# A fused cross-attention and FFN kernel on one core: four reorderings around GEGLU, CROSS2 and FFN

## The reference

```python
# first block: 16 heads of 64
x = attn(LN(x), LN(x), Wq1, Wk1, Wv1, Wo1, bo1) + x          # SELF
x = attn(LN(x), context, Wq2, Wk2, Wv2, Wo2, bo2) + x        # CROSS
h = LN(x) @ Wp + bp;  a, gate = split(h, 2)
x = (a * gelu(gate)) @ Wf + bf + x                           # GEGLU
# second block: 16 heads of 8
out = attn8(x @ Wq + bq, context @ Wk + bk, context @ Wv + bv) @ Wo + bo    # CROSS2
out = out + gelu(LN(out) @ W1 + b1) @ W2 + b2                # FFN
return x + out
```

## Time and profile before

| | |
|---|---|
| median of 3 runs | 451.03 us (450.54 to 451.25) |
| the profiled execution's own time | 450.97 us |
| its span, first to last instruction | 449.3 us |
| TensorE matmuls (PE) | 434.4 us, 97% of the span |
| VectorE (DVE) | 352.9 us, 79% |
| ScalarE (ACT) | 318.8 us, 71% |
| GpSimd (POOL) | 201.8 us, 45% |
| granted TensorE clock | 1.00, the higher of its two levels (2.4 GHz) |

### The profile page before, as it was taken

One profiled execution on the slowest core, in us unless ns is written; L12 is line 12 of the kernel. 1 busy time (PEld: TensorE's weight loads), 2 busy tenths in 40 slices (PEclk: granted clock), 3 DMA queues, 4 the chain that ended last, 5 costly groups with the idle time before them and its releaser, 6 DMA issues.

```text
span 449.3 us, 17107 instructions
## 1 busy us (share of the span) xinstructions
PE 434.4 (97%) x7513; PEld 399.4 (89%) x7513; DVE 352.9 (79%) x649; ACT 318.8 (71%) x587; POOL 201.8 (45%) x226
## 2 busy tenths in 40 slices
PE   8999999999999999999999999999999999999897
PEld 7979999898999999989989899889999777778797
DVE  4888889688797887978978789896784788898471
ACT  5686676777778768787677776876546576777763
POOL 1883332555345634555352533523342232152782
PEclk9999999999999999999999999999999999999999
DMA  7202021110200000000000000000000000000011
GB/s 230 58 4 85 3 85 28 53 48 4 63 4 4 10 3 11 12 3 10 12 2 12 3 10 13 3 3 1 2 1 19 10 12 19 4 1 4 13 36 47
DMA packets 14623, 10.61 MB, mean 24 GB/s; under 512 B 5188, under 2 KB 13592, under 8 KB 14552
## 3 DMA queue, kind: packets, MB, share of 16 engines
q1 hardware_dynamic: 14120, 9.48, 7.3%
q10 hardware_dynamic: 432, 0.07, 0.1%
HBM read 8.50 MB, written 1.05 MB: 21 GB/s over the span
## 4 chain that ended last, share of the span: by engine, by line
PE 88%; DVE 6%; ACT 2%; issue 2%; POOL 1%; DMA 1%; POOLq 0%
PE stage L683 12%; PE stage L684 11%; PE stage L685 11%; PE scp L865 8%; PE scp L788 7%; PE scp L837 6%; PE scp L944 6%; PE out0p L885 4%; PE out0p L913 4%; PE out0p L887 3%; PE out0p L886 3%; PE stage L849 3%; PE scp L805 2%; DVE pr L1417 1%; PE stage L934 1%
## 5 line engine op out<-in xcount | busy, mean ns | idle before, releaser
L1734 POOL TENSOR_TENSOR pr<-pr,rc 128x1024 f32<-128x1024 f32 (+1 forms) x32 | 59.1, 1867 | 76.5 <-DVE rc L1447 76.4
L1165 ACT ACTIVATE pr<-pr 128x1024 f32<-128x1024 f32 x48 | 50.8, 1059 | 36.7 <-DVE pr L1417 30.1
L1672 POOL TENSOR_TENSOR rstd<-veps,neghalf 128x2 f32<-128x2 f32 x32 | 22.8, 714 | 70.8 <-DVE veps L1365 70.6
L1099 ACT ACTIVATE vt<-stage 64x512 f32<-64x512 f32 x83 | 49.2, 592 | 4.8 <-PE stage L685 1.2
L1461 DVE COPY vt<-stage 64x512 f32<-64x512 f32 x45 | 31.2, 694 | 21.8 <-PE stage L685 20.9
L1412 DVE TENSOR_REDUCE mx<-scp 128x16 f32<-128x1024 f32 x32 | 39.2, 1224 | 8.9 <-PE scp L788 8.5
L1099 ACT ACTIVATE ot_h<-scp 128x512 fp32r<-128x512 f32 x64 | 33.4, 600 | 13.3 <-PE scp L865 13.3
L1467 DVE TENSOR_TENSOR ot_r<-scp,ot_h 128x512 fp32r<-128x512 f32 x64 | 40.0, 683 | 2.3 <-ACT ot_h L1099 1.0
L1099 ACT ACTIVATE k_of_heads<-stage 128x512 f32<-128x512 f32 x62 | 36.9, 598 | 5.4
L1417 DVE TENSOR_TENSOR pr<-scp,mx 128x1024 f32<-128x1024 f32 x32 | 39.2, 1224 | 1.1
L1445 DVE TENSOR_REDUCE sm<-pr 128x16 f32<-128x1024 f32 x32 | 38.0, 1188 | 0.0
(11 more groups left out here) (266 smaller groups left out, 1398.8 us busy)
## 6 DMA issues: line engine op xcount, KB each, us to landing
ctx_in<-in_ctx_dram SPq DMA_DIRECT2D x16, 96.0 KB, 2.0
masked_k<-in_L_xattn_Wo_dram SPq DMA_DIRECT2D x2, 512.0 KB, 3.8
out_dram<-rows SPq DMA_DIRECT2D x8, 128.0 KB, 1.8
rows<-in_x_dram SPq DMA_DIRECT2D x1, 768.0 KB, 9.4
pr<-in_L_xattn_Wq_dram SPq DMA_DIRECT2D x1, 512.0 KB, 4.9
pr<-in_L_xattn_Wk_dram SPq DMA_DIRECT2D x1, 512.0 KB, 6.2
pt<-in_L_xattn_Wv_dram SPq DMA_DIRECT2D x1, 512.0 KB, 7.6
rows<-in_L_xattn_Wq_dram SPq DMA_DIRECT2D x1, 512.0 KB, 5.1
```

The costliest lines, as they stand in the source:

```text
L1099: return nc.scalar.activation(dst, s, ACT.Copy)
L1165: nc.scalar.activation(pr[t][:, :], pr[t][:, :], ACT.Exp, scale=scale[s.phase]).then_inc(exped, 1)
L1734: nc.gpsimd.tensor_tensor(p, p, rc[:, t, h:, None].to_broadcast([ROWS, H - h, N]), ALU.mult)\
```

## The change

Four edits. In the class `Counts` and in TensorE's `seventh_cross2_group`, v of the last group goes ahead of the transposes. TensorE's GEGLU groups are written out (`written=(GEGLU,)`). In VectorE's GEGLU group 6 the copy of x for CROSS2's group 1 goes ahead of parts 2 and 3 of the up projection (the p_step of parts 1 to 3 is split after part 1). On GpSimd, the bias of FFN's group 1 moves from CROSS2's last group to FFN's group 0, and there it stands behind the rest of group 2 and the power of group 3, which also change places.

```diff
@@ Counts.group, CROSS2's group 6
                 self.qk(p, g + 1)
+                self.use("v", p, g + 1)
                 for i in (0, 1):
                     self.use("pt", p, g, i)
-                self.use("v", p, g + 1)
@@ each_group
-        def each_group(eng, body, looks_far=False):
+        def each_group(eng, body, looks_far=False, written=()):
...
-                lead, tail = 2, (4 if looks_far or p == CROSS2 else 2)
+                lead, tail = 2, (4 if looks_far or p == CROSS2 or p in written else 2)
@@ TensorE, seventh_cross2_group
                 cross2_out_step(before, 1)
+                v_step(one, s)
                 cross2_turn_step(s, 0)
-                v_step(one, s)
                 cross2_scores_step(one, s)
@@ TensorE
-            each_group(pe, group)
+            each_group(pe, group, written=(GEGLU,))
@@ VectorE, group
                     if s.phase == GEGLU:
-                        p_step(one, (1, 2, 3))
+                        p_step(one, (1,))
+                    if s.is_group(GEGLU, GROUPS - 2):
+                        norm_step(s.ahead(3), two)
+                    if s.phase == GEGLU:
+                        p_step(one, (2, 3))
                     if three:
                         norm_step(three, two)
-                    if s.is_group(GEGLU, GROUPS - 2):
-                        norm_step(s.ahead(3), two)
                     down_step(s)
@@ GpSimd, group, CROSS2's group 7
                     norm_step(s.ahead(3), two)
                     bias_step(one)
+                    return
+                if s.is_group(FFN, 0):
+                    rest_step(two)
+                    rstd_step(three)
+                    bias_step(one)
                     bias_step(two)
                     return
```

## The result

| | before | after |
|---|---|---|
| median of 20 runs each, on one chip | 450.3 us (449.55 to 451.63) | 452.05 us (450.08 to 454.62) |
| the profiled execution's own time | 450.97 us | 452.35 us |
| its span | 449.3 us | 450.6 us |
| mean granted TensorE clock in it | 1.000 | 0.996 |

The account below looks back on a forecast made before the run. TensorE, busy 434.4 of 449.3 us, was taken as the bound. The terms -0.45 - 0.40 + 0 + 2.0 = +1.15 us on the profiled 450.97 gave 452.1 us, with a range of 451.2 to 452.9.

Parts of the forecast that it names:

- x copied earlier: TensorE's 0.42 us wait ahead of L694 goes and CROSS2's first scores start earlier: gain 0.45 us, bounds 0.3 and 0.49.
- v ahead of the transposes: In CROSS2, v fills TensorE's 0.92 us hole and scores start earlier: gain 0.40 us, bounds 0.25 and 0.62.
- GEGLU written out: TensorE's GEGLU loop, 4.87 us a group without idle time: removing its branch gains 0.
- up projection 2 to 3, full clock: In FFN, the rest of group 3 starts 5.03 us after that of group 2, delaying TensorE: cost 1.60 us.
- drift in FFN, full clock: Later FFN groups lose 0.17 us in each of three rounds, 0.5 at most: taken as 0.4 us.
- The likeliest case: The forecast within its own bounds, 451.5 to 452.6 us, slower by FFN's GpSimd order: chance 0.68.
- the circle: In FFN, VectorE and GpSimd's round of power, normalizing pair, add, statistics: 3.60 us against TensorE's 3.43 a group.
- GpSimd's term: GpSimd's new order in FFN: 1.60 us plus drift 0.4, cost 2.0 us, bounds 1.6 and 2.2.
- (b): Rival: GpSimd's late work before FFN's rest of group 3 costs nothing, only gains stand: 450.1 us, chance 0.07.
- (c): Rival: writing out GEGLU gains by two branches, 0.75 us each: 450.6 us, chance 0.02.
- (a): Rival: gains larger or FFN's cost smaller, nearly cancelling: beyond the bounds down to 451.0 us, chance 0.13.
- (d): Rival: one instruction stall in the shifted program (+0.75 us), or the circle drifts faster: 452.9 us, chance 0.10.

Follow-up runs that it names:

- x_copy: Only VectorE's copy of x moved one place forward, against the kernel before: 450.72 us, ratio 0.9988 (0.9972 to 1.0005).
- v_ahead: Only v of the last CROSS2 group put ahead of the transposes, against the kernel before: 450.4 us, ratio 0.9986 (0.9973 to 1.0000).
- written: Only TensorE's GEGLU groups written out, against the kernel before: 450.96 us, ratio 1.0005 (0.9993 to 1.0017).
- pool_filled: Only GpSimd's edit, plus 6 and 4 resultless identity matmuls in TensorE's two waits, against the kernel before: 453.82 us, ratio 1.0056.
- pool_only: Only GpSimd's new order in FFN's first groups, against the kernel before: 453.25 us, ratio 1.0048 (1.0028 to 1.0068).
- rest_first: Only the rest of group 2 and power of group 3 swapped, group 1's bias left in CROSS2, against the kernel before: 453.27 us, ratio 1.0059.
- no_pool: The three other edits without GpSimd's, against the kernel before: 450.2 us, ratio 0.9986 (0.9973 to 0.9998).
- bias_late: Only group 1's bias and residual moved behind the rest of group 2, power of group 3 still ahead, against the kernel before: 452.85 us, ratio 1.0037.
- rest_first_filled: Rest of group 2 ahead of group 3's power, plus 6 and 4 identity matmuls in TensorE's two holes, against the kernel before: 453.36 us, ratio 1.0047.

## Why the prediction was right, and where it was off

Forecast were 452.1 us and a slower kernel; measured were 452.05 us and a ratio of 1.0035. The two times agree better than the steps do, since 450.3, the median of before in the result's own runs, was 0.7 us below the one that the sum was made against. That part is luck: the forecast of +1.15 on 450.3 would have been 451.45, and the fall of the clock, which was not forecast, filled the gap. Step by step:

| step | forecast | measured |
|---|---|---|
| x copied earlier | -0.45 (0.3 to 0.49) | -0.41, after and x_copy |
| v ahead of the transposes | -0.40 (0.25 to 0.62) | -0.46, after and v_ahead |
| GEGLU written out | 0 | 0: groups of 4.87 us; written 1.0005 |
| up projection 2 to 3, full clock | +1.60 (5.03 us) | +1.62 (5.05 us), pool_filled |
| drift in FFN, full clock | +0.4 | +0.28, pool_filled |
| the clock | not in the sum | about +1.4 us in half of the runs |

**Right.** The direction, the place and the mechanism. The likeliest case took place: the rest of group 2 gained nothing by being put first, since it had waited for ScalarE (GpSimd's idle time ahead of it grew from 1.05 to 3.33 us), and the three instructions it overtook came back between the rests. At full clock the sum of the measured terms is -0.41 - 0.46 + 0 + 1.90 = +1.03 us (forecast +1.15), and the runs of after at full clock are 0.8 us above before. The drift was smaller, since the pace of the circle was read from one round of 3.60 us; the next one in the same trace takes 3.52 (432.84 to 436.36), and so do those of pool_filled. That is 0.09 a round over TensorE's 3.43, three times which is the measured 0.28.

**Off.** The step that was mis-sized is GpSimd's term, for the sentence that x of group 3 comes late by "0.5 to 1.3, inside the 1.60, not on top". The lateness was at its upper end and a little beyond it: in after TensorE's up projection 2 started 1.53 us earlier than before (422.56 against 424.09) and its transposes 0.18 us earlier (424.70 against 424.88), so they were 1.35 us late. As time that is indeed inside the term (pool_filled: 5.05 us, no more). But it also put a wait of 1.20 us right behind the one of 1.64, and in that place TensorE's clock fell to half in the profiles of the three kernels that have both waits. Of their 36 runs 20 had a mean clock of 0.996 or 0.992 (after 11 of 20, pool_only 5 of 10, rest_first 4 of 6); that it fell at the same place in those without a profile is inferred. None did in the 13 runs of the two kernels in which the waits were filled, and of the kernels without the second wait there, with the one of about 1.65 us (no_pool, written, bias_late, x_copy, v_ahead), at most one run each (of 11 or 12) had a lower mean, and that was 0.999. In the profiled execution this makes the stretch 6.33 us instead of 5.05, and with that the term 2.91 us instead of 1.90; of the drift nothing is to be seen there, since TensorE itself was later than the circle of VectorE and GpSimd.

I also had the x of group 3 as the lesser chain. rest_first_filled shows the chain over VectorE nearly as long as the one of the rests (4.85 against 5.05 us), so the cost would not have gone away with the bias put back. What the forecast left out of it is that the late pair also delays the statistics of group 4, and with them the power that stands ahead of the rest of group 3.

**The rivals.** (b), that GpSimd's late work costs nothing, fell with pool_only (1.0048). (c), that writing out gains by the branches, fell with written. (a), that the terms nearly cancel, is near what a run at full clock shows, 0.8 us above before, but the terms themselves were inside their bounds, and the clock takes it away on the median. (d) named a stall for instructions or a faster drift; the loss beyond the sum came from neither of them.

**Open.** Why the totals do not follow FFN more closely: the two filled kernels spend about 1 us more outside it than before, bias_late 0.7 more, and pool_only at full clock 0.7 less than pool_filled's 1.90 would make it. The place and the size of a term are therefore shown by the distances in the traces, and by the totals only that there is a loss. Filling the waits kept the clock up but did not shorten the total, so that the fall costs about 1.4 us rests on comparing runs of one kernel by their clock. Why the clock falls in half of the runs and not in the others, whose instructions are the same: there is a profile of one execution of each kernel only, and the others show only their mean clock.

## What to carry to other kernels

In an in-order queue, an instruction that waits for another engine gains nothing by being put ahead of ones that are ready; their length, less what idle time stood there, is handed to the next one behind it, so count the queue from one deadline to the next. Look instead for the head of the chain that is late (here two transposes that stood behind a wait they did not need): moving that gained 0.9 us alone, where moving the tail lost 1.9 us in FFN. A second short wait close to a first one on TensorE can cost more than its length, since the clock can fall; read the granted clock of the windows behind it, and compare runs by their clock.

## What the runs showed of the hardware

In the profile of after the clock fell near the end of the second of two waits, of 1.64 and 1.20 us with 0.94 us of matmuls between them (the 0.44 and 0.50 of the windows of 422 to 424), and it stayed at half for 3.4 us in after and for 6.8 us in rest_first; the same 16 matmuls of the down projection took 1.95 us at full, 2.66 at partly half and 3.62 at half clock. With the wait of 1.65 us but not the one of 1.20, no run of the five kernels had a mean below 0.999. TensorE's pair of transposes takes 0.38 us at full clock and 0.69 at half.

VectorE's pair of normalizing instructions took 1.47 us at 423.18 beside a busy GpSimd, and 0.60 when it was alone. The Trainium skill gives a cause ("SBUF — State Buffer", Who interferes with whom): a VectorE instruction that uses both ports and a GpSimd one shut each other out for the length of the one that came first. The two rows agree with it, though no run here tests it against another cause. It makes the chain over x of group 3 longer, for in the old order this pair met an idle GpSimd.
